# Attention softmax on one Trainium2 core: the exponential reads the scores from PSUM head by head, with the negated maximum as its bias

## What is computed

```python
q = heads(norm(x) @ Wq + bq)              # 16 heads, 128 tokens
k, v = heads(ctx @ Wk + bk), heads(ctx @ Wv + bv)   # 16 heads, 77 tokens
s = q @ k.T                               # 128 x 77 for each head
p = exp(scale * s - scale * max(s)) / sum # softmax over the 77 tokens
x = x + tanh(gate) * ((p @ v) @ Wo + bo)  # scale = head size ** -0.5
```

## Time and profile before

| | |
|---|---|
| time, median of 3 runs | 1367.64 us (1365.57 to 1368.13) |
| profiled execution, span of its instructions | 1365.9 us (this is the time the profile gives for it; 1.7 us under the median) |
| busy PE / DVE / ACT / POOL | 1141.5 / 1007.3 / 643.4 / 373.1 us |
| attention of layer 0 (`heads8`) | about 37 to 205 us, a group every 44.8 us |
| attention of layer 1 (`heads64`) | about 490 to 690 us, a group every 52 to 54 us |
| attention of layer 3 (`heads8`) | about 1107 to 1281 us |
| granted PE clock, mean | 0.874 of 2.4 GHz |

### The profile page before, as it was taken

The page is one execution under the profiler, slowest core; times in us unless marked ns, Lnnn a source line. Parts: engine busy times, 40 slices in busy tenths (PEclk is TensorE's granted clock), DMA queues, the critical chain, the costliest instruction groups (busy, mean ns, idle before and its releaser), DMA issues.

```text
span 1365.9 us, 19983 instructions
## 1 busy us (share of the span) xinstructions
PE 1141.5 (84%) x6317; PEld 921.1 (67%) x6317; DVE 1007.3 (74%) x2437; ACT 643.4 (47%) x1226; POOL 373.1 (27%) x265
## 2 busy tenths in 40 slices
PE   3888987989889789999966488999999968988665
PEld 2777885767667568878844266767676657877655
DVE  7777767887888866676658876778788787787643
ACT  2555554654656354655510011656665535554344
POOL 5563551222222321211200200111121243444200
PEclk9888988999999899999987655899999969888877
DMA  3010100000000100000000021000000000000000
GB/s 93 32 31 0 31 16 12 1 12 0 15 0 1 29 30 1 0 0 0 1 1 0 0 63 31 1 1 0 0 0 0 0 16 1 0 0 0 1 16 16
DMA packets 22491, 15.54 MB, mean 11 GB/s; under 512 B 3690, under 2 KB 19817, under 8 KB 22441
## 3 DMA queue, kind: packets, MB, share of 16 engines
q1 hardware_dynamic: 22441, 14.90, 3.6%
HBM read 13.85 MB, written 1.05 MB: 11 GB/s over the span
## 4 chain that ended last, share of the span: by engine, by line
PE 60%; DVE 16%; issue 14%; POOL 5%; ACT 3%; DVEq 0%; DMA 0%; POOLq 0%; ACTq 0%; SPq 0%
PE banks L734 7%; PE banks L736 6%; PE banks L735 6%; PE banks L838 5%; PE banks L774 5%; PE banks L921 5%; PE banks L923 4%; PE banks L922 4%; PE banks L913 3%; PE banks L995 3%; POOL kbd L410 2%; PE banks L1004 2%; PE banks L1014 2%; DVE xn L1209 2%; POOL sh L418 2%
## 5 line engine op out<-in xcount | busy, mean ns | idle before, releaser
L1466 DVE TENSOR_TENSOR hlo<-hf,hhi 128x512 fp32r<-128x512 f32 x256 | 194.7, 792 | 6.5
L418 POOL TENSOR_TENSOR sh<-sh,rd 128x616 f32<-128x616 f32 x96 | 116.6, 1217 | 273.2 <-DVE rd L1254 273.1
L609 ACT ACTIVATE hf<-banks,b 128x512 f32<-128x512 f32 x256 | 170.8, 695 | 8.9 <-PE banks L736 8.6
L394 POOL TENSOR_TENSOR rstd<-vv,const 128x4 f32<-128x4 f32 x32 | 32.4, 1012 | 407.2 <-DVE vv L1201 407.2
L530 ACT ACTIVATE sh<-sh 128x308 f32<-128x308 f32 x192 | 81.1, 460 | 126.8 <-DVE sh L1244 126.8
L467 POOL TENSOR_TENSOR acc<-acc,yw 128x512 f32<-128x512 f32 x56 | 79.7, 1424 | 210.4 <-DVE yw L1473 210.4
L838 PE MATMUL banks<-prob,v 128*128 128x128 f32 x1024 | 122.8, 279 | 0.0
L838 PEld LDWEIGHTS banks<-prob,v 128*128 128x128 f32 x1024 | 120.2, 196 | 0.8
L774 PE MATMUL banks<-const,sh 128*77 128x128 f32 x768 | 115.9, 301 | 4.2 <-POOL sh L418 4.2
L518 ACT ACTIVATE prob<-banks 77x512 f32<-77x512 f32 x192 | 99.8, 586 | 21.5 <-PE banks L774 21.5
L1239 DVE TENSOR_REDUCE top_s<-banks 128x4 f32<-128x308 f32 x192 | 83.9, 469 | 34.9 <-PE banks L995 17.6
(11 more groups left out here) (327 smaller groups left out, 2548.5 us busy)
## 6 DMA issues: line engine op xcount, KB each, us to landing
raw<-in_L_ffn_W SPq DMA_DIRECT2D x16, 512.0 KB, 3.8
out<-x SPq DMA_DIRECT2D x4, 256.0 KB, 2.2
x<-in_x SPq DMA_DIRECT2D x1, 768.0 KB, 4.5
raw<-in_L_xattn_Wq SPq DMA_DIRECT2D x1, 512.0 KB, 3.5
raw<-in_L_ffn_expert_w SPq DMA_DIRECT2D x1, 512.0 KB, 3.9
wo<-in_L_xattn_Wo SPq DMA_DIRECT2D x1, 512.0 KB
ctok<-in_ctx SPq DMA_DIRECT2D x1, 462.0 KB
raw<-in_L_xattn_Wk SPq DMA_DIRECT2D x1, 384.0 KB, 3.3
```

What stands on the lines that cost most here:

```text
L418: pool.tensor_tensor(e_, e_, r_, ALU.mult).then_inc(hs.prob, 1)
L609: act.activation(hf[:, u % 4, :], ps[:, u % 4, :], func, bias=b1[:, u:u + 1])\
L1466: dve.tensor_tensor(hlo[e % 2][:, c, :], hf[:, u % 4, :], f32(hhi[e % 2][:, c, :]), ALU.subtract).then_inc(ff.split, 1)
```

## The change

The subtraction goes. The maximum is taken with its sign turned; a small DVE instruction multiplies these four values of a unit by the scale (`neg_s`, 128 x 4), and the exponential reads the scores in PSUM itself, as exp(scale * s + neg). As a bias is one value for each partition, and each head has its own maximum, a unit now takes four exponentials of 77 columns in place of one of 308. The bank of a unit is free when its last exponential has read it, so PE's waits on `sub` become waits on `exp`. `sub` now counts the small multiplications. The order of all other work stays.

```diff
+        neg_s = place("neg_s", [P, H], F32, s)
...
 # ACT
                     for u in units:
                         act.wait_ge(hs.sub, 4 * (4 * G + i) + u + 1)
-                        e_ = sh[i % 2][:, u, :, :].rearrange("p h t -> p (h t)")
-                        act.activation(e_, e_, ACT.Exp, scale=scale).then_inc(hs.exp, 1)
+                        for h_ in range(4):
+                            ins = act.activation(sh[i % 2][:, u, h_, :], ps[:, u % 2, h_ * SP:h_ * SP + SK], ACT.Exp,
+                                                 scale=scale, bias=neg_s[:, 4 * u + h_:4 * u + h_ + 1])
+                        ins.then_inc(hs.exp, 1)
...
 # PE
                             if i:
-                                pe.wait_ge(hs.sub, n - 2 + u + 1)
+                                pe.wait_ge(hs.exp, n - 2 + u + 1)
                             scores(G, i, u).then_inc(hs.s, 1)
...
-                            pe.wait_ge(hs.sub, n + u - 1)
+                            pe.wait_ge(hs.exp, n + u - 1)
                             scores(G, i, u).then_inc(hs.s, 1)
...
 # DVE
-            def attend(hs, G, add, prepare=None):
+            def attend(hs, G, scale, add, prepare=None):
...
-                                dve.tensor_reduce(top_s[:, 4 * u:4 * u + 4].unsqueeze(2), s_, AX.X, ALU.max)\
+                                dve.tensor_reduce(top_s[:, 4 * u:4 * u + 4].unsqueeze(2), s_, AX.X, ALU.max, negate=True)\
                                    .then_inc(hs.max, 1)
                             for u in (2 * pair, 2 * pair + 1):
-                                s_ = ps[:, u % 2, 0:4 * SP].rearrange("p (h t) -> p h t", h=4)[:, :, 0:SK]
                                 dve.wait_ge(hs.max, n + u + 1)
-                                dve.tensor_tensor(sh[i % 2][:, u, :, :], s_,
-                                                  top_s[:, 4 * u:4 * u + 4].unsqueeze(2).to_broadcast([P, 4, SK]),
-                                                  ALU.subtract).then_inc(hs.sub, 1)
+                                dve.tensor_scalar(neg_s[:, 4 * u:4 * u + 4], top_s[:, 4 * u:4 * u + 4], scale, None,
+                                                  ALU.mult).then_inc(hs.sub, 1)
```

More of the change, by code:

```diff
@@ L1311, in heads8 @@
                 with dve.Fori(0, NG - 1) as g:
-                    attend(h8, g + NG * run, add, lambda between: blocks(g + 1, between))
+                    attend(h8, g + NG * run, D8 ** -0.5, add, lambda between: blocks(g + 1, between))
                     front_c(g + NG * phase + 2)
-                attend(h8, NG - 1 + NG * run, add)
+                attend(h8, NG - 1 + NG * run, D8 ** -0.5, add)
             def second_biases(s_):
@@ L1540, in heads64 @@
                 with dve.Fori(0, NG - 1) as g:
-                    attend(h64, g, add, lambda between: blocks(g + 1, between))
+                    attend(h64, g, D64 ** -0.5, add, lambda between: blocks(g + 1, between))
                     front_c(g + 2 * NG + 2)
-                attend(h64, NG - 1, add)
+                attend(h64, NG - 1, D64 ** -0.5, add)
             def mixed():
```

## The result

The changed kernel takes 1437.34 us (median of 4 runs, 1434.22 to 1440.63), the kernel before 1366.77 us beside it: a ratio of 1.0519 with a 95% interval of 1.0496 to 1.0541, so it is 5.2% slower. The direction was forecast; the size was not: +70.6 us in place of +33.4, and outside the range of 1384 to 1430 us. One run further down (1406.95 us, of the version with sums from ACT and the earlier normalising) was over 1.5% longer than the fastest of its kernel; its version's median and ratio leave it out.

The account below looks back on a forecast made before the run. The DVE, ACT, DVE loop was taken to bound heads8, growing from 3.08 to 3.74 us a pair: 26.9 us there plus 6.5 us in heads64 gave 1367.6 + 33.4 = 1401 us. The range was 1384 to 1430 us.

Parts of the forecast that it names:

- What bounds the kernel: In heads8, a serial DVE, ACT, DVE loop of 3.08 us a pair sets the pace, with 0.55 us spare a tile.
- The two multiplications: In the loop on DVE, multiplications of 0.17 us replace the subtractions; 0.20 us in place of 0.51, loop -0.31 us.
- POOL's share: In a heads8 group POOL is busy 24 of 44.8 us, so it is not late.
- Eight small exponentials: In the loop on ACT, eight of 77 columns take 1.82 us in place of 0.85, loop +0.97 us.
- Rival 1: On ACT, small exponentials start 0.25 us apart, the loop is 4.02 us and the time 1422 us; chance 0.15.
- PE's later release: PE's scores wait for exponentials; the next tile's scores stay just hidden, by some 0.2 us.
- rival 2: In heads8, PE's clock may rise later after more waits; 1415 us, at most 1430; chance 0.08.
- heads64: In these four groups PE is nearly gapless and the loop has room; +1.6 us a group, 6.5 us in all.
- Rival 3: In the loop, the shorter DVE part wins if exponentials start under about 0.13 us apart; 1363 us; chance 0.04.

## Why the prediction was wrong

- **What bounds the kernel**: right for `heads8`. The loop of DVE, ACT and DVE set the pace, and what was added to it showed in the time. `heads64` has room: with the multiplication put into the kernel before, its four groups took 116.3 us from their first to their last reciprocals in place of 115.2, though 18 of 32 first multiplications were held up there.
- **The two multiplications, "0.20 us in place of 0.51"**: this step failed. From the start of the multiplications to that of the exponentials it was 0.66 us, so the loop lost 0.15 us here where 0.31 was to be gained. The 0.17 us of the earlier trace rows is the operation with POOL idle. In the loop POOL starts its half of the probabilities 0.28 us after the reciprocal starts (105.04, 105.32), 1.21 us long, and the multiplication starts 0.90 us after the reciprocal, within it. The term was mis-sized by 0.46 us in an ordinary pair and more where POOL makes keys; 20 of the 96 pairs were free of it. In all it is 37 to 39 us, by the mean of the 192 and by the run with the maxima in PSUM. POOL's hold on DVE stood at nothing in the sum.
- I used POOL's share (24 of 44.8 us) to dismiss it. That answers whether others wait for its results, and not whether it holds something that they need. The trace of before had the warning, in the normalising instructions at 118.57 above, which take 0.34 us in `heads64`; I looked at the operation's price only where nothing ran beside it.
- **Eight small exponentials**: 1.82 forecast, 1.83 us measured. Rival 1, starts 0.25 us apart, did not come: they are 0.21 us apart.
- **PE's later release**: I had worked out its cover with 3.6 us for the values pass, where the earlier trace rows has 3.79, which leaves no cover. With the maxima in PSUM one step in seven is longer than the loop, 3.9 to 4.05 us; so little came of it. I did not test it by itself.
- **The clock (rival 2)**: it came in part. In the changed kernel PE fell back to 1.2 GHz inside the `heads8` group shown, after PE had done only two matmuls of scores from 116.5 to 117.8 us. The granted clock from 117 to 122 us is 0.66, and the values pass at 117.81 us took 5.44 us in place of 3.79. The reciprocals around it stay 4.25 us apart, so the loop hid it; 0.75 us was lost between this group and the next (21.99 us from its last reciprocal to the next first one, 21.24 in its neighbours). The mean clock, 0.871 against 0.874, does not show this. With the maxima in PSUM that group has no such second stretch. How much of the 38.8 us is the clock's no run separates.
- **heads64**: 1.6 us a group forecast. From the first reciprocal of its second group to that of its third, the timelines give 52.6 us in the kernel before (548.17 to 600.73), 54.5 with the maxima in PSUM (563.33 to 617.84), and 56.0 in the changed kernel (578.45 to 634.42). The term was about right there (1.9; the other two such distances give 2.7 and 1.7), and the port came on top of it here as well.
- **The range** had no term for an interaction between engines; its upper end came from ACT's prices (rival 1) and PE's clock (rival 2). Rival 3 needed exponentials under 0.13 us apart, and they are 0.21.

## What to carry to other kernels

When an edit puts an instruction into a loop, look up what each other engine does at that moment, and price the instruction from a row in which POOL was busy, not from the cleanest one. A small `tensor_scalar` from SBUF to SBUF, or a `tensor_tensor` with both inputs in SBUF, costs up to the length of POOL's instruction beside it; a reciprocal or a `tensor_reduce` did not. Reading from PSUM, folding the constant into an earlier pass, or moving it to a moment when POOL waits avoided this. Replacing two large ACT instructions by eight with a bias more than doubled their time here (0.85 to 1.83 us), so the work removed elsewhere must be worth about a microsecond a pair.

## What the hardware showed that I had not expected

- A `tensor_scalar` or `tensor_tensor` of 128 x 4 in SBUF took 0.14 to 0.97 us (up to 2.01 us in the version with the subtraction between). The long ones ended 0.02 to 0.03 us after POOL's running instruction; POOL's own (1.21 and 2.26 us) were not lengthened. With its input in PSUM it took at most 0.164 us. Reciprocals and sums from SBUF to SBUF were not held up.
- ACT's instructions without a per-partition operand started 0.16 us apart at 77 columns from SBUF and at 128 from PSUM; with a bias 0.21 us at 77 from PSUM.
- Reading an accumulator is an instruction that adds 0.09 us to each exponential.
